# A decoder's attention heads: the first two groups' loads issued by ScalarE and SyncE in place of GpSimd

## What is computed

```python
# self attention: t = 512 keys, causal
scores = jnp.einsum('bqhd,bkhd->bhqk', q, k) * SCALE + causal_bias
out = jnp.einsum('bhqk,bkhd->bqhd', softmax(scores), v)
# cross attention: 1601 keys, key mask
scores = jnp.where(mask[:, None, None, :] == 0, neg_inf, jnp.einsum('bhqd,bhkd->bhqk', Q, K) * SCALE)
out = jnp.einsum('bhqk,bhkd->bhqd', softmax(scores), V)
```

## Time and profile before

| | |
|---|---|
| median of 3 runs | 2289.7 us (2285.7 to 2290.43) |
| the profiled execution | 2287.91 us, its span 2286.1 us |
| mean granted clock of TensorE | 0.914 |
| first matmul of the self attention's heads | 1132.14 us |
| first matmul of the cross attention's heads | 1556.08 us |

### The profile page before, as it was taken

The page is one execution under the profiler, slowest core; times in us unless marked ns, Lnnn a source line. Parts: engine busy times, 40 slices in busy tenths (PEclk is TensorE's granted clock), DMA queues, the critical chain, the costliest instruction groups (busy, mean ns, idle before and its releaser), DMA issues. The chain is left out here.

```text
span 2286.1 us, 31725 instructions
## 1 busy us (share of the span) xinstructions
PE 1921.4 (84%) x12188; PEld 1094.6 (48%) x12188; DVE 1408.9 (62%) x2349; ACT 1057.6 (46%) x1670; POOL 529.4 (23%) x689
## 2 busy tenths in 40 slices
PE   8879588888569999993799988864999999998677
PEld 4777455555458888882323336530222222222445
DVE  1431233344457777765477746677899999993744
ACT  1110132233135655551156662321788888888342
POOL 0530000000034444431323401232011111100453
PEclk9999799999579999995879999985999999999798
DMA  3000446654266666633411104542011011100200
GB/s 115 1 1 1 175 173 223 223 198 149 83 272 236 266 244 258 254 114 100 130 26 30 34 14 154 173 126 60 15 31 30 22 24 30 30 16 1 83 10 29
DMA packets 107659, 237.43 MB, mean 104 GB/s; under 512 B 28026, under 2 KB 79774, under 8 KB 104032
## 3 DMA queue, kind: packets, MB, share of 16 engines
q1 hardware_dynamic: 83108, 200.41, 24.5%
q0 software_dynamic: 23872, 31.71, 5.2%
q10 hardware_dynamic: 528, 3.28, 0.4%
HBM read 180.06 MB, written 54.69 MB: 103 GB/s over the span
## 5 line engine op out<-in xcount | busy, mean ns | idle before, releaser
L1431 DVE TENSOR_REDUCE Eh_maxima<-Eh_max 128x2 f32<-128x802 f32 x512 | 474.9, 987 | 30.2 <-PE Eh_max L1316 25.6
L1419 ACT ACTIVATE Eh_probs<-Eh_pair 128x1024 f32<-128x1024 f32 (+1 forms) x288 | 287.8, 999 | 124.9 <-PE Eh_pair L1355 124.8
L1316 PE MATMUL Eh_max<-Eh_KS,Eh_QS 49*128 49x401 f16 x1024 | 198.0, 357 | 70.6 <-DVE Eh_maxima L1431 39.6
L805 PE MATMUL C_y<-C_x_high,C_W 128*128 128x256 f16 x1472 | 249.9, 273 | 1.5 <-DVE C_x_low L1051 1.5
L1378 PE MATMUL Eh_av_ps<-Eh_probs,E_V 128*17 128x512 f32 (+1 forms) x1664 | 223.0, 609 | 0.1
L805 PE MATMUL C_y<-C_x_low,C_W 128*128 128x256 f16 x736 | 201.3, 274 | 0.0
L1431 DVE TENSOR_REDUCE Dh_maxima<-Dh_max 128x2 f32<-128x1024 f32 x128 | 152.1, 1222 | 51.2 <-PE Dh_max L1324 49.3
L1316 PEld LDWEIGHTS Eh_max<-Eh_KS,Eh_QS 49*128 49x128 f16 x1024 | 50.5, 94 | 258.8 <-DVE Eh_maxima L1431 198.2
L1419 ACT ACTIVATE Eh_probs<-Eh_single 128x512 f32<-128x512 f32 x272 | 161.5, 594 | 18.8 <-PE Eh_single L1355 18.7
L805 PEld LDWEIGHTS C_y<-C_x_high,C_W 128*128 128x128 f16 x1472 | 144.5, 98 | 18.8 <-issue 1.9
L1273 POOL DMA_DIRECT2D Eh_KS<-E_kd x64 | 38.7, 605 | 390.9 <-PE Eh_pair L1355 386.1
(11 more groups left out here) (332 smaller groups left out, 3531.4 us busy)
## 6 DMA issues: line engine op xcount, KB each, us to landing
C_W<-w_split SPq DMA_DIRECT2D x23, 3072.0 KB, 11.3
S_w<-in_w_experts_dram SPq DMA_DIRECT2D x32, 768.0 KB, 8.6
w_split<-S_parts SPq DMA_DIRECT2D x32, 768.0 KB, 6.0
Eh_KS<-E_kd POOLq DMA_DIRECT2D x64, 150.1 KB, 3.3
C_tail<-in_expert_tail_dram SPq DMA_DIRECT2D x23, 384.0 KB, 8.4
B_ctxT<-in_ctxT_dram SPq DMA_DIRECT2D x4, 1601.0 KB
B_ctxN<-in_ctx_dram SPq DMA_DIRECT2D x4, 1536.0 KB
E_ctxT<-in_ctxT_dram SPq DMA_DIRECT2D x12, 384.0 KB, 4.5
```

Source lines behind the costliest of these rows:

```text
L805: last = mm(y_ps[n % Y_BANKS][:, i, :], W[:, u, a, at_w:at_w + P], x[:, s % 2, k, :], start=(q == 0), stop=(q == len(parts) - 1))
L1316: last = self.nc.tensor.matmul(bank[:, a, 0:self.cw], self.QS[r, slot, p, qt * P:(qt + 1) * P], self.KS[r, slot, p, k0:k0 + self.cw], star ...
L1419: self.nc.scalar.activation(dst, src, ACT.Exp, scale=1.0 / SCORE).then_inc(self.exp_done, 1)
L1431: self.nc.vector.tensor_reduce(self.maxima[:, g % 2, :, p * TPB + qt, c], self.max_ps[n % 2][:, :, 0:self.cw], AX_X, ALU.max).then_inc(sel ...
```

## The change

Groups 0 and 1 (`EARLY = 2`) are loaded by the other two engines that can issue DMAs. They have semaphores of their own, `early_loaded[0]` and `early_loaded[1]`.

- SyncE issues units 2 and 3 of group 0 ahead of the four constant loads, and units 2 and 3 of group 1 behind them.
- ScalarE issues, ahead of its first exponential, the mask rows (in Eh) and units 0 and 1 of group 0, then the same of group 1.
- GpSimd begins with group 2.
- TensorE waits for `early_loaded` for groups 0 and 1, and for `loaded` with fewer turns from then on.

The number, the size and the targets of the loads are the same.

```diff
+EARLY = 2
...
+        self.early_loaded = [sem(f"early_loaded{i}") for i in range(EARLY)]
...
+    def load_pair(self, queue, g, u, signal):
+        slot = g % self.slots
+        p, a = divmod(u, 2)
+        for dst, src in ((self.KS, self.kd), (self.QS, self.qd)):
+            queue.dma_start(dst[a * HALF:a * HALF + STACK, slot, p, :],
+                            src[:, g * STRIPS + u:g * STRIPS + u + 1].rearrange("g u d s -> g (u d) s")).then_inc(signal, 16)
+
+    def load_mask(self, queue, g, signal):
+        slot = g % self.slots
         if not self.causal:
             for a in range(2):
-                sp.dma_start(self.KS[a * HALF + STACK:a * HALF + STACK + 1, slot], self.mask_rows[g * STRIPS // H]).then_inc(self.loaded[slot], 16)
+                queue.dma_start(self.KS[a * HALF + STACK:a * HALF + STACK + 1, slot], self.mask_rows[g * STRIPS // H]).then_inc(signal, 16)
+
+    def await_load(self, pe, g):
+        if g < EARLY:
+            pe.wait_ge(self.early_loaded[g], self.loads)
+        else:
+            pe.wait_ge(self.loaded[g % self.slots], len(range(g, EARLY - 1, -self.slots)) * self.loads)
...
     def sync(self, sp):
+        self.load_pair(sp, 0, 2, self.early_loaded[0])
+        self.load_pair(sp, 0, 3, self.early_loaded[0])
...
+        for u in range(2, STRIPS):
+            self.load_pair(sp, 1, u, self.early_loaded[1])
         for g in range(GROUPS):
             self.load_rows(sp, g)
 
     def pool(self, pool):
-        for g in range(GROUPS):
+        for g in range(EARLY, GROUPS):
             self.load(pool, g)
...
     def scalar(self, act):
+        for g in range(EARLY):
+            self.load_mask(act, g, self.early_loaded[g])
+            for u in range(2):
+                self.load_pair(act, g, u, self.early_loaded[g])
```

More of the change, by code:

```diff
@@ L1270, in load @@
         for u in range(STRIPS):
[L1271 to L1274, removed]
+            self.load_pair(sp, g, u, self.loaded[slot])
+        self.load_mask(sp, g, self.loaded[slot])
+    def load_pair(self, queue, g, u, signal):
[6 more added lines that the diff above has]
+        slot = g % self.slots
         if not self.causal:
             for a in range(2):
-                sp.dma_start(self.KS[a * HALF + STACK:a * HALF + STACK + 1, slot], self.mask_rows[g * STRIPS // H]).then_inc(self.loaded[slot], 16)
+                queue.dma_start(self.KS[a * HALF + STACK:a * HALF + STACK + 1, slot], self.mask_rows[g * STRIPS // H]).then_inc(signal, 16)
[4 more added lines that the diff above has]
+            pe.wait_ge(self.loaded[g % self.slots], len(range(g, EARLY - 1, -self.slots)) * self.loads)
     def load_rows(self, sp, g):
@@ L1309, in maxima_of @@
         if i == 0:
-            pe.wait_ge(self.loaded[slot], self.turn_of(g) * self.loads)
+            self.await_load(pe, g)
         if n >= 2:
```

## The result

| | before | after |
|---|---|---|
| median | 2289.18 us (2285.7 to 2290.51, 6 runs) | 2304.48 us (2301.58 to 2308.92, 6 runs) |
| ratio | | 1.007, 95% interval 1.0057 to 1.0084 |
| profiled execution, its span | 2287.91, 2286.1 | 2308.92, 2307.1 |
| Dh's opening, in two profiles | 7.94, 7.88 | 12.84, 13.35 |
| Eh's opening, in two profiles | 9.25, 9.06 | 17.71, 17.18 |

The change made the kernel slower, as forecast, but by nearly three times the forecast 5.6 us, and the time lies above the range. An opening is here, and in all that follows, the time from SyncE's first issue of a heads' stage to the start of TensorE's first weight load for the maxima.

The account below looks back on a forecast made before the run. The landing of group 0's loads and constant rows was taken to bound both openings; transfer, GpSimd and semaphore terms summed to +2.9 us in Dh and +2.7 in Eh, 5.6 us slower, median 2295.3 us, range 2287 to 2301.

Parts of the forecast that it names:

- The spread: Group 0's hardware-queue loads use 3 engines in Dh and 6 in Eh, always the same ones; stages lose 5.6 us.
- The faster rival: Hardware queues spread group 0's loads over all engines, so issuing limits both openings; 5.5 us faster, 2284 us, chance 0.13.
- Issue: SyncE and ScalarE issues at both openings take 0.5 us each, hidden, so no engine's compute pays for them.
- the first packet: At both openings, the first data packet moves 0.9 us after SyncE's first issue.
- Dh's sum: Self attention opening: TensorE starts at 1135.05 against 1132.14 us, +2.9 us, bounds +1.0 to +5.2.
- Eh's sum: Cross attention opening: TensorE starts at 1558.8 against 1556.08 us, +2.7 us, bounds +0.8 to +5.1.
- its term for GpSimd: In Eh's opening, GpSimd's third group, coming at the same time, adds 1.7 us, from 0 to 3.5.
- The crowding rival: In both openings, ScalarE's group 1 loads take full turns beside SyncE's constants; +11.5 us, 2301 us, chance 0.09.
- The clock: TensorE's half-clock stretch after the start could give back or cost 1 us; nothing taken, 1 us kept either way.
- The signs to look for: First maxima 9.5 to 13 us (Dh), 10 to 14.5 (Eh) after SyncE's first issue; about 3 and 6 engines; GpSimd landing about 3 us.

Follow-up runs that it names:

- g0_alone: Changed kernel with only group 0 on SyncE and ScalarE, GpSimd's later loads held until the first scores; openings 11.3 us in Dh, 11.6 in Eh.
- wide_alone: Changed kernel with loads by row, only group 0 on SyncE and ScalarE, GpSimd held until the first scores; openings 8.0 us in Dh, 10.0 in Eh.
- the doses: Changed kernel, GpSimd issuing none, one, two or all four strips of group 2 before waiting for first scores; Eh openings 12.1, 13.6, 14.2, 17.4 us.
- pool_late: Changed kernel with all GpSimd loads held until the first maxima matmul is done; openings 11.7 us in Dh, 12.1 in Eh.
- best: Changed kernel, loads by row, constants before SyncE's half, only group 0 on SyncE and ScalarE, GpSimd held until first scores; 2288.92 against 2290.53 us, ratio 0.9998.

## Why the prediction was right in direction and wrong in size

**The spread: right.** The reading from a constant load of five packets was that a load goes on as many engines as it has parts, always the same ones. It holds for the 48-row loads: 3.3 engines and a nearly flat 66 to 74 GB/s in `g0_alone`, and twice the share with the loads by row. The trace's semaphore events count it too. Group 0's semaphore in the changed kernel gets 32 updates in Dh and 60 in Eh; with the loads by row 128 and 76. The Trainium skill says in DMA: Bandwidth & Descriptors, section "Why a DMA increments its semaphore by 16 and not by 1", that on a hardware queue each engine used adds one, and the issuing sequencer adds the rest in one step. By that rule 32 is 8 x (3 + 1), 60 is 8 x (6 + 1) and four for the two mask rows, 128 is 8 x 16, and 76 is 8 x (8 + 1) + 4. The trace agrees: 3, 6, 16 and 8 engines. The faster rival (the loads spread, 2284 us) is refuted by this. In the form of `wide_alone` it could be tried, and gave not 5.5 us but nothing: the openings were 8.0 and 10.0 us. Its reading of the loads was not what failed there: in Dh group 0 landed at 4.4 us. Its sum had the constants landing 5 to 6 us after SyncE's first issue (1129.2 to 1130.2), and they landed at 8.0.

**Issue: off the path in the sum, but not free.** The forecast took 0.5 us an issue; a 48-row load took 0.68 to 0.91 us on SyncE. It hid behind the narrow transfer. What I left out is the first packet: I took 0.9 us from a constant load that needs 0.34 us to issue, and for a 48-row load it came at 1.6. That is 0.7 us in Dh. In Eh the mask rows move at 0.9 us, and the first packet of a 48-row load is again at 1.6.

**Dh's sum: +2.9 forecast, +5.2 measured**, at the edge of its bound of +5.2. Term by term, from `g0_alone`: the first packet 1.6 for 0.9; group 0 (8.9 + 10.5) / 3 = 6.5 for 5.9, since ScalarE's half took 54 ns a packet; the constants 2.0 for 1.7 (12 of their 16 packets lie on the three low engines, 8.0 us x 12/16 / 3); 1.1 for 0.8 from the last packet's end to the start. Those add up to its opening of 11.3 us. On top come 0.4 for group 1, which I had at nothing, and 1.4 for 1.6 for GpSimd. So the mechanism held, and several small terms were each a little too small. The terms of `g0_alone` are arithmetic from packet times, not tested by a kernel of their own; the other two are differences of two kernels.

**Eh's sum: +2.7 forecast, +8.3 measured. This is the step that failed, and its term for GpSimd most of all.** I put the third group's cost at 1.7 us, the middle between nothing and its engine time of 3.5 us per engine. Holding it back took 5.3 us away, and the doses show it growing with the bytes. The bound was wrong in kind, since it held nothing but GpSimd's own engine time. That was 22.8% of 16 x 17.6 us = 64 us, 4.0 per engine if it is spread evenly, and beyond it the packets that TensorE waited for got slower per byte (58 us per MB in place of 48; over 1.41 MB and six engines 2.3 us). This estimate, 4.0 + 2.3 = 6.3, is 1.0 us over the measured 5.3, so how much of either really lay on the path is not shown. In the worst part of the opening, 1561 to 1564 us, GpSimd's queue held two thirds of the engine time, and the hardware queues moved 0.14 MB in 3 us, 47 GB/s; here the changed kernel, in order of share, and behind it `pool_late` from 1551 to 1556, where they moved 0.67 MB in 5 us, 134 GB/s:

```profile
q0 software_dynamic: 174, 0.43, 67.7%
q10 hardware_dynamic: 40, 0.13, 21.9%
q1 hardware_dynamic: 9, 0.01, 2.2%
...
q1 hardware_dynamic: 161, 0.33, 18.7%
q10 hardware_dynamic: 152, 0.34, 18.2%
```

The other 3 us of Eh's opening are the narrow loads (1.6), the order of the constants (0.8) and group 1 (0.5), against 1.0 in the forecast without GpSimd. In the forecast's own terms, `g0_alone` has 0.7 us more to the first packet and about 0.7 more for the packets (the last ends 10.9 us after the first issue).

Why the same company costs 6.4 us per MB in Eh and 1.9 in Dh stays open. The rows show what differs: in Dh the hardware queues' packets took 31.5 us for 0.59 MB with GpSimd beside them and 32.3 for 0.65 MB without, 53 and 50 us per MB, so they were hardly stretched. In Eh, GpSimd's packets are larger (0.83 MB in 575 packets against 0.75 in 1191). No kernel changed the size of the packets alone.

**The crowding rival (+11.5 us, 2301)** came close in size and is refuted in its mechanism: without group 1 on those queues the openings were 0.4 and 0.5 us shorter, where it wanted 2.9 and 3.

**The clock.** Nothing was taken for it, 1 us kept either way. From TensorE's start in Dh to Eh's barrier it was 414.7 and 413.8 us before and 416.5 and 415.7 after; that is 1.9 us more on average, and the sum of the openings leaves 1.8 of the 15.3 us. Whether the clock made these was not tested.

**The signs to look for.** TensorE's start 12.8 us after SyncE's first issue in Dh was within 9.5 to 13; 17.7 us in Eh was beyond 10 to 14.5. The shares of about 3 and 6 engines were right once the queues ran alone (20.7% in `g0_alone`, 36.9% in the rows of `pool_late` above), and too high for the changed kernel's first 5 us (11% in Dh and 16% in Eh). GpSimd's loads landed after 5.7 us in Eh, not 3: that sign told of the failed term.

## What to carry to other kernels

Before a load is moved from GpSimd to SyncE or ScalarE, count on how many engines it will lie there, and what already lies on the same ones: here, with group 0 alone, the loads with 3 and 6 parts in their slowest dimension made the openings 3.1 and 1.6 us longer than the same bytes ordered by row. Ask next what the freed queue will bring at once. Work that comes sooner than it is needed is not free when it shares engines with work that is waited for; with an unknown company, bound its cost from above by its whole engine time plus the slowing of the others, and do not take the middle. And an issue that leaves a busy queue helps only as far as the next thing that the consumer waits for: `wide_alone` had group 0 there 3.4 us sooner and then waited for the constants, and `best` stood where the kernel before stood.

## What the runs showed that was not expected

- A 48-row load took SyncE 0.68 to 0.91 us and ScalarE 0.69 to 1.32 us to issue, GpSimd 0.59 us in the median; a constant load took 0.24 to 0.34 us in the kernel before and 0.27 to 0.66 behind the 48-row loads. On the free engines each issue was slower than in the queue it came from. The Trainium skill says in DMA: Bandwidth & Descriptors, section "Issuing engines are not separate DMA queues", that issuing from several engines only saves issue time, since all share the same 16 DMA engines. That they share them, the trace confirms: holding GpSimd's queue back took 5.3 us off Eh's opening. That issue time is saved holds for Dh's eight loads together, out after 3.5 us in place of 5.5, but the two openings became 13.5 us longer by how the transfers were spread and by what ran beside them.
- With GpSimd's queue beside them, the packets of the other two queues took longer per byte in Eh (58 against 48 us per MB), and in Dh hardly (53 against 50).
- The same kernel's clock rose 44 us after its first matmul in Dh in one profile and 36 us in the next.
